# A two-layer block on one core: another order on ScalarE in the first normalisation, and query and key rows stored three deep in stack order

## The chip, the cores and the metric

The kernel runs on one core of a Trainium2 chip. The metric is the device time of one execution in microseconds (us), smaller being better. Before the change the median of three runs is 2131.8 us.

## What is computed

Two layers work on 2 x 512 tokens of width 512 in float32. Layer 0 is an attention with 32 heads of 16 channels and a gated feed-forward network, both on the same normalised input; layer 1 is a state-space mixer and a linear layer with low-rank additions. The change lies at the start of layer 0:

```python
def _layernorm(x, axis=-1, eps=1e-05):
    m = jnp.mean(x, axis=axis, keepdims=True)
    v = jnp.var(x, axis=axis, keepdims=True)
    return (x - m) / jnp.sqrt(v + eps)
...
    q, k, v = (proj(w_q), proj(w_k), proj(w_v))
    scores = jnp.einsum('bhqd,bhkd->bhqk', q, k) / jnp.sqrt(jnp.float32(D_K))
    attn = jax.nn.softmax(scores, axis=-1)
    out = jnp.einsum('bhqk,bhkd->bhqd', attn, v)
...
    xn = _layernorm(x, axis=-1)
    x = x + _L0_attn_ref(xn, ...) + _L0_ffn_ref(xn, ...)
    xn = _layernorm(x, axis=-1)
    x = x + _L1_attn_ref(xn, ...) + _L1_ffn_ref(xn, ...)
```

## The kernel before

The program is five blocks one after the other, each with its own instruction list for every engine: normalisation with the q, k and v products (`emit_qkv`), attention with the gate and up products, the down products with the second normalisation, the state-space mixer, and the output products. Lists are written out by hand, and semaphores alone set when an instruction may run. An engine takes its list in order, so an instruction that waits holds up all behind it. SyncE (SP) issues all the transfers, on one queue.

Float32 products are made of three fp32r products: every operand is split into a high and a low part, and `product` (L154 to L158) adds low x high, high x low and high x high.

**First normalisation** (`FirstNorm`). Tokens come in 8 tiles of 128. For tile t VectorE finds mean and variance (`moments`), ScalarE takes the root (`root`, L217), VectorE makes reciprocal and shift (`scalars`), ScalarE scales the tile (`normalise`, L222), TensorE turns it into PSUM in 4 matmuls (`turn`, L210), ScalarE copies the high part out (`high`, L227) and VectorE the low part (`low`, L255). In step t of ScalarE's list stand root(t), normalise(t-1) and high(t-2), and from step 4 on the split of a weight tile. TensorE's list is: turn 0 to 4, wait for the low part of tile 3, the first 12 products of weight tile 0, turn 5, turn 6, the first 12 products of tile 1, turn 7, wait for the low part of tile 7, and then all other products.

**q, k and v.** There are 12 weight tiles of 256 KB: 8 for q and k in turn (n even is q), then 4 for v. A q or k tile gives 128 channels x 1024 tokens. ScalarE writes its high part to `qk_hi` (`hi`, L503), VectorE its low part to `qk_lo` (L522), both with 3 buffers; then SP writes the two parts of 512 KB each to the scratch tensor `qk_parts` in DRAM (`parts(n)`, L427). ScalarE may fill a buffer again when the writes of the tile three earlier have landed.

**Stacks.** The scores of four heads are made from a stack: two halves of 48 partitions, each of 3 rows of 16 channels (q: high, high, low; k: high, low, high), so that one matmul over 48 partitions adds the three products. `Stacks.stack` (L319) fills one of 4 buffers from `qk_parts` with 12 transfers of 64 KB, one for each row, half and side. There are 16 stacks: 3 are loaded in the first block, right behind `parts(1)`, `parts(2)` and `parts(3)`; the first of them waits until `parts(0)` and `parts(1)` have landed (L432). The others are loaded during attention.

SP's list in the first block is thus: 8 tiles of x, weight tiles 0 to 2, a table of vectors, and then in step n the load of weight tile n and, from n = 6 on, parts(n-6) with the stack behind it. The weights of v (tiles 8 to 11) stand behind parts(1), parts(2), parts(3) and parts(4). At the end come parts(6), parts(7), and two weight tiles of the next block.

TensorE's products of v follow those of q and k: for each of 8 token tiles 12 products, then two row steps (`row_step`, L332; 4 matmuls of L341), from which VectorE takes the row maxima (L351). The first row step waits for the low part of the eighth q/k tile.

Of the kernel before, what the change touches and what calls it, by code (L numbers as in the profile page):

```python
# [13 lines left out]
F32 = mybir.dt.float32  # L14
# [5 lines left out]
P = 128  # L20
B, L, D = 2, 512, 512
T = B * L
KT = D // P
# [52 lines left out]
def after(eng, sem, value):  # L76

    if not isinstance(value, int) or value > 0:
        eng.wait_ge(sem, value)
# [81 lines left out]
class FirstNorm:  # L161
# [66 lines left out]

    def scalar(self, act, feed):
        for t in range(NTOK + 2):  # L230
            if t < NTOK:
                self.root(act, t)
            if 1 <= t <= NTOK:
                self.normalise(act, t - 1)
            if t >= 2:
                self.high(act, t - 2)
            if 4 <= t < 4 + feed.begun:
                feed.split_hi(act, 0, t - 4, 0)

# [55 lines left out]
class Stacks:  # L295
# [23 lines left out]
    def stack(self, sp, c, it, i):  # L319

        n = it * NB + i
        after(sp, self.key_sum, (n - NB + 1) * 16)
        r = it * P + i // 2 * 64
        for row, dst, side, part in ((0, self.qs, 0, 0), (1, self.qs, 0, 0), (2, self.qs, 0, 1),
                                     (0, self.ks, 1, 0), (1, self.ks, 1, 1), (2, self.ks, 1, 0)):
            for half in range(2):
                src = c.qk_rows[part, side, bass.ds(r + half * 2 * DK, 2 * DK), i % 2 * L:(i % 2 + 1) * L]
                at = half * HALF + row * DK
                sp.dma_start(dst[at:at + DK, i, :, :].bitcast(F32),
                             src.rearrange("(h d) t -> d h t", h=2)).then_inc(self.stacked[i], 16)  # L330

    def row_step(self, pe, rows, it, i, u, deep):  # L332

        n = it * NB + i
        if u == 0:
            pe.wait_ge(self.stacked[i], (it + 1) * 12 * 16)
        after(pe, self.max_done, n * 8 + (u - deep + 1))
        qt = u % 4
        for half in range(2):
            at = slice(half * HALF, half * HALF + KSTACK)  # L340
            mm = pe.matmul(rows[:, u % deep, half, :], self.qs[at, i, u // 4, qt * P:(qt + 1) * P],  # L341
                           self.ks[at, i, u // 4, :], start=True, stop=True)
        mm.then_inc(self.row_sum, 1)
# [50 lines left out]
def emit_qkv(nc, c, w, x_load, xhi, xlo, st, feed, tile_done, next_feed):  # L394
# [3 lines left out]
    with ExitStack() as ctx:  # L398
# [23 lines left out]
        @block.sync  # L422
        def _(sp):
            def parts(n):
                sp.wait_ge(qk_l, n + 1)
                for part, src in enumerate((qk_hi, qk_lo)):
                    sp.dma_start(c.qk_dram[part, n % 2 * KT + n // 2], src[:, n % NR, :].bitcast(F32)  # L427
                                 ).then_inc(parts_out[n % NR], 16)
                if n == 1:
                    for s in parts_out[0:2]:  # L430
                        sp.wait_ge(s, 32)
                    sp.wait_ge(st.cleared, 2)  # L432
                if 1 <= n < NB:
                    st.stack(sp, c, 0, n - 1)
            norm.load(sp)
            feed.begin_load(sp)
            norm.load_vectors(sp)
            for n in range(3 * KT):
                if n >= feed.begun:
                    feed.load(sp, w, W_QKV + n, 0, n)  # L440
                if n >= S + 2:
                    parts(n - S - 2)
            for n in range(3 * KT - S - 2, nqk):
                parts(n)
            next_feed.begin_load(sp)
            st.neg_max(sp, 0, 0)
            sp.wait_ge(norm.vec_in, 16)
            for i, s in enumerate(parts_out):
                sp.wait_ge(s, len(range(i, nqk, NR)) * 32)

        @block.tensor
        def _(pe):
# [45 lines left out]
        @block.scalar  # L498
        def _(act):
            def hi(n):  # L500
                act.wait_ge(tile_done, n + 1)
                after(act, parts_out[n % NR], n // NR * 32)
                act.activation(qk_hi[:, n % NR, :], ps[:, n % 3, :, :].rearrange("p b t -> p (b t)"),  # L503
                               ACT.Copy, scale=scale[n]).then_inc(qk_h, 1)
            norm.scalar(act, feed)
            for n in range(3 * KT):
                if n >= feed.begun:
                    feed.split_hi(act, 0, n, n // feed.raw_slots)
                if n >= S:
                    hi(n - S)  # L510
            for t in range(NTOK):
                act.wait_ge(v_sum, t + 1)
                act.activation(v[:, t, :], pv[:, t % 2, :], ACT.Copy).then_inc(v_out, 1)
                if t == HELD:
                    st.high(act, ptr, 0, 0)
                    next_feed.begin_hi(act)
# [1597 lines left out]
def build(nc, w, vec, x_rows, x_out, upto=99):  # L2114
    c = Constants()
    c.vec_dram, c.x_rows = vec, x_rows
    scratch = lambda n, s: nc.dram_tensor(n, s, F32).ap()
    c.qk_dram = scratch("qk_parts", (2, 2 * KT, P, T))
    c.qk_rows = c.qk_dram.rearrange("a (s n) p t -> a s (n p) t", s=2)
    c.att_dram = scratch("att_sums", (2, D, T))  # L2120
    c.x1_dram = scratch("x_mid", (P, KT, T))
    c.cum_dram = scratch("dt_sums", (NTOK, 2, H, CS))
# [100 lines left out]
```

## Time and profile before

| | before |
|---|---|
| median of 3 runs | 2131.8 us (2131.57 to 2133.14) |
| profiled execution, its own time | 2133.82 us |
| its span, first to last instruction | 2132.1 us |
| granted TensorE clock, mean | 0.992 |
| busy: TensorE, VectorE, ScalarE, GpSimd | 98%, 69%, 63%, 41% |
| moved by the DMA engines | 305.34 MB, mean 143 GB/s |

Engines are named as the profile names them: PE is TensorE (PEld its weight loads), DVE VectorE, ACT ScalarE, POOL GpSimd, SP SyncE. A row of the timeline gives the start, the duration, the engine and the source line, the tile written and the tiles read, and in brackets how long the engine had been idle and what ended that. PEclk is the granted clock as a share of 2.4 GHz. The DMA share is the mean busy share of 16 DMA engines. The first block ends at about 107 us of the span, attention at about 400 us.

### The profile page before, as it was taken

To read this page: it belongs to the slowest core of one execution; us is meant where nothing else is said; L and a number is where in the kernel's file an instruction comes from. 1 tells how busy PE (TensorE), PEld (TensorE's weight loads), DVE (VectorE), ACT (ScalarE), POOL (GpSimd) and SP (SyncE) were. 2 spreads that over 40 slices of the span, in tenths; PEclk is the share of its full clock that TensorE was granted. 3 is DMA by queue.
4 is the path that set the end of the run, shared out by engine and by line. 5 is a ranking of instruction groups with operands and counts; after the bars stand their busy time and mean duration, and the time that the engine had idled before them with its cause. 6 is when DMAs were issued, how large, how long until landed. Compare 5 with 4: busy or idle time off the path is not lost.

```text
span 2132.1 us, 33690 instructions
## 1 busy us (share of the span) xinstructions
PE 2081.6 (98%) x12040; PEld 1550.1 (73%) x12040; DVE 1462.3 (69%) x1811; ACT 1337.6 (63%) x2376; POOL 869.6 (41%) x762
## 2 busy tenths in 40 slices
PE   7899999998999999999999999999999999999999
PEld 5644444486777777777777777777777767888887
DVE  4466666285578778778878788687787775555555
ACT  4255555543587877888878787887878783333322
POOL 1011110130157666666757667675766682000000
PEclk9999999999999999999999999999999999999999
DMA  4422222241545555545545545555455467444452
GB/s 158 158 81 74 73 79 62 70 151 55 124 139 166 167 152 163 165 144 171 156 153 171 161 149 161 158 164 161 155 159 167 149 190 257 153 148 148 144 183 89
DMA packets 182781, 305.34 MB, mean 143 GB/s; under 512 B 20416, under 2 KB 96704, under 8 KB 182496
## 3 DMA queue, kind: packets, MB, share of 16 engines
q1 hardware_dynamic: 182624, 303.29, 45.8%
q8 instruction: 94, 1.54, 0.3%
q14 instruction: 63, 0.52, 0.1%
HBM read 249.90 MB, written 53.06 MB: 142 GB/s over the span
## 4 chain that ended last, share of the span: by engine, by line
PE 71%; ACT 2%; DVE 1%; POOL 1%; issue 1%; DMA 1%; DVEq 0%; SPq 0%; POOLq 0%; ACTq 0%
PE ssm_pp L156 16%; PE ssm_pp L158 15%; PE ssm_pp L157 15%; PE ssm_py L1444 5%; PE ssm_py L1439 4%; PE ssm_pstate L1423 4%; PE ssm_turn L1400 2%; PE ssm_py L158 1%; PE ssm_py L157 1%; PE ssm_py L156 1%; PE ssm_pp L1383 1%; PE ssm_pstate L158 1%; PE ssm_pstate L157 1%; PE ssm_pstate L156 1%; PE ssm_turn L158 1%; PE ssm_turn L157 1%
## 5 line engine op out<-in xcount | busy, mean ns | idle before, releaser
L156 PE MATMUL ssm_pp<-xhi,ssm_lo 128*128 128x512 f32 x1192 | 479.4, 402 | 4.2 <-DVE ssm_bc L1668 3.5
L158 PE MATMUL ssm_pp<-xhi,ssm_hi 128*128 128x512 f32 x1192 | 466.0, 391 | 0.0
L157 PE MATMUL ssm_pp<-xlo,ssm_hi 128*128 128x512 f32 x1192 | 465.7, 391 | 0.0
L1556 ACT ACTIVATE ssm_sct<-ssm_cumb,ssm_gpar 128x128 f32<-128x128 f32 x1024 | 313.1, 390 | 72.0 <-DMA ssm_cumb<-dt_sums 48.7
L148 POOL TENSOR_TENSOR ssm_lo<-ssm_raw,ssm_hi 128x512 fp32r<-128x512 f32 x150 | 244.1, 1633 | 92.5 <-ACT ssm_hi L137 92.5
L156 PEld LDWEIGHTS ssm_pp<-xhi,ssm_lo 128*128 128x128 f32 x1192 | 224.0, 188 | 67.5 <-issue 18.7
L1668 DVE SCALAR_TENSOR_TENSOR ssm_xc<-ssm_pp,vectors,ssm_xc 128x1022 f32<-128x1022 f32 (+2 forms) x192 | 245.2, 1277 | 36.2 <-ACT ssm_xc L1510 31.5
L158 PEld LDWEIGHTS ssm_pp<-xhi,ssm_hi 128*128 128x128 f32 x1192 | 224.2, 188 | 48.2
L157 PEld LDWEIGHTS ssm_pp<-xlo,ssm_hi 128*128 128x128 f32 x1192 | 224.3, 188 | 42.7
L1703 DVE TENSOR_TENSOR ssm_sct<-ssm_sct,ssm_cbm 128x1024 f32<-128x1024 f32 x128 | 228.4, 1785 | 27.7 <-ACT ssm_sct L1563 27.7
L1845 POOL TENSOR_TENSOR ssm_go<-ssm_t,ssm_gt 128x512 f32<-128x512 f32 x128 | 165.0, 1289 | 172.1 <-DVE ssm_t L1739 172.1
L767 ACT ACTIVATE att_pt<-att_keys 128x512 f32<-128x512 f32 x256 | 143.9, 594 | 136.0 <-PE att_keys L657 135.8
L2035 ACT ACTIVATE xlo<-ssm_gt 128x1024 fp32r<-128x1024 f32 x64 | 67.8, 1060 | 238.9 <-PE ssm_turn L158 228.1
L351 DVE TENSOR_REDUCE stk_mx<-att_rows 128x2 f32<-128x1024 f32 x112 | 137.3, 1226 | 90.5 <-PE att_rows L341 90.5
L148 POOL TENSOR_TENSOR ffn_lo<-ffn_raw,ffn_hi 128x512 fp32r<-128x512 f32 x33 | 42.9, 1301 | 375.8 <-ACT ffn_hi L137 375.8
L1715 DVE TENSOR_TENSOR ssm_xp<-ssm_turn,ssm_gpar 128x512 f32<-128x512 f32 x128 | 87.8, 686 | 151.2 <-PE ssm_turn L1400 151.2
L1444 PE MATMUL ssm_py<-ssm_sct,ssm_xp 128*64 128x128 f32 x2048 | 184.3, 274 | 0.0
L2072 DVE TENSOR_TENSOR xlo<-ssm_gt,xlo 128x1024 fp32r<-128x1024 f32 x64 | 78.4, 1225 | 149.2 <-ACT xlo L2035 149.2
L1822 POOL TENSOR_TENSOR ssm_xw<-ssm_xp,ssm_gpar 128x512 f32<-128x512 f32 x96 | 127.2, 1325 | 110.3 <-DVE ssm_xp L1715 110.2
L1439 PE MATMUL ssm_py<-ssm_cecl,ssm_state 128*64 128x128 f32 x1536 | 154.1, 279 | 0.1
L1739 DVE SCALAR_TENSOR_TENSOR ssm_t<-ssm_xc,vectors,ssm_py 128x128 f32<-128x128 f32 x512 | 142.4, 336 | 5.3 <-PE ssm_py L1444 5.3
L1444 PEld LDWEIGHTS ssm_py<-ssm_sct,ssm_xp 128*64 128x64 f32 x2048 | 124.5, 137 | 24.3 <-DVE ssm_xp L1715 18.2
(287 smaller groups left out, 4151.4 us busy)
## 6 DMA issues: line engine op xcount, KB each, us to landing
ssm_cumb<-dt_sums SPq DMA_DIRECT2D x96, 1024.0 KB, 5.9
ssm_raw<-w SPq DMA_DIRECT2D x150, 256.0 KB, 5.6
gated<-ssm_go SPq DMA_DIRECT2D x128, 256.0 KB, 4.3
ssm_cumb<-dt_sums SPq DMA_DIRECT2D x32, 512.0 KB, 4.0
ssm_gt<-w SPq DMA_DIRECT2D x64, 256.0 KB, 2.7
ssm_xc<-gated SPq DMA_DIRECT2D x32, 512.0 KB, 4.2
ssm_sct<-gated SPq DMA_DIRECT2D x32, 512.0 KB, 4.3
ffn_raw<-w SPq DMA_DIRECT2D x37, 256.0 KB, 2.8
```

The costliest lines, as they stand in the source:

```text
L148: i = dve.tensor_tensor(lo, src, hi, ALU.subtract)
L156: pe.matmul(out, wlo, xhi, start=start, stop=False)
L157: pe.matmul(out, whi, xlo, start=False, stop=False)
L158: return pe.matmul(out, whi, xhi, start=False, stop=stop)
L767: act.activation(pt[:, kt % 2, PAIRED[u % HQ], :], keys[:, u % 2, :], ACT.Exp).then_inc(exp_done, 1)
L1439: pe.matmul(p_y[r * HP:(r + 1) * HP, s % 2, ct, :], state[:, ch % 2, h * HP:(h + 1) * HP], cecl[:, s % 2, h, :], start=True, stop=False)
L1444: mm = pe.matmul(p_y[r * HP:(r + 1) * HP, s % 2, ct, :], xp[:, s % 2, h * HP:(h + 1) * HP], sct[:, s % 2, h, :], start=(ch == 0), stop=True)
L1556: i = act.activation(sct[:, s % 2, h, :], cumb[:, s % 2, 0, h, :], ACT.Relu, scale=-1.0, bias=gpar[:, unit, 0, s % NTOK, h:h + 1])
L1668: i = dve.scalar_tensor_tensor(dst[:, :, sh:L], pp[:, e % 2, :, 0:L - sh], col(conv_col(g, e) + tap), dst[:, :, sh:L], ALU.mult, ALU.add)
L1703: dve.tensor_tensor(sct[:, s % 2, :, :], sct[:, s % 2, :, :], cbm[:, s % NTOK, :].unsqueeze(1).broadcast_to([P, HU, CS]), ALU.mult).then_i ...
L1739: i = dve.scalar_tensor_tensor(t2[:, s % 2, ct, :], xc[:, s // NTOK, ct, t * CS:(t + 1) * CS], col(g * (2 * CU) + (V_D + s // NTOK * CU + ...
L1845: pool.tensor_tensor(go[:, s % 2, :, :], t2[:, s % 2, :, :], gt[:, s // NTOK, :, t * CS:(t + 1) * CS], ALU.mult).then_inc(g_done, 1)
```

## The change

In ScalarE's list of the first normalisation, high(t-2) now stands ahead of root(t) and normalise(t-1). The scratch tensor becomes `(2 * KT, P // DK, 3, DK, T)`: for each tile and head the three rows of the stack lie one behind the other. `parts(n)` writes the high part twice, so 3 writes of 512 KB in place of 2, and a stack is filled by 4 transfers of 192 KB over 48 partitions in place of 12 of 64 KB over 16. Counts that are waited for follow.

```diff
--- before.py
+++ after.py
@@ -228,12 +228,12 @@
 
     def scalar(self, act, feed):
         for t in range(NTOK + 2):
+            if t >= 2:
+                self.high(act, t - 2)
             if t < NTOK:
                 self.root(act, t)
             if 1 <= t <= NTOK:
                 self.normalise(act, t - 1)
-            if t >= 2:
-                self.high(act, t - 2)
             if 4 <= t < 4 + feed.begun:
                 feed.split_hi(act, 0, t - 4, 0)
 
@@ -320,20 +320,19 @@
 
         n = it * NB + i
         after(sp, self.key_sum, (n - NB + 1) * 16)
-        r = it * P + i // 2 * 64
-        for row, dst, side, part in ((0, self.qs, 0, 0), (1, self.qs, 0, 0), (2, self.qs, 0, 1),
-                                     (0, self.ks, 1, 0), (1, self.ks, 1, 1), (2, self.ks, 1, 0)):
+        for side, dst in enumerate((self.qs, self.ks)):
             for half in range(2):
-                src = c.qk_rows[part, side, bass.ds(r + half * 2 * DK, 2 * DK), i % 2 * L:(i % 2 + 1) * L]
-                at = half * HALF + row * DK
-                sp.dma_start(dst[at:at + DK, i, :, :].bitcast(F32),
-                             src.rearrange("(h d) t -> d h t", h=2)).then_inc(self.stacked[i], 16)
+                src = c.qk_heads[side, bass.ds(it * (P // DK) + (i // 2 * HQ + half * 2), 2), :,
+                                 i % 2 * L:(i % 2 + 1) * L]
+                at = half * HALF
+                sp.dma_start(dst[at:at + KSTACK, i, :, :].bitcast(F32),
+                             src.rearrange("h q t -> q h t")).then_inc(self.stacked[i], 16)
 
     def row_step(self, pe, rows, it, i, u, deep):
 
         n = it * NB + i
         if u == 0:
-            pe.wait_ge(self.stacked[i], (it + 1) * 12 * 16)
+            pe.wait_ge(self.stacked[i], (it + 1) * 4 * 16)
         after(pe, self.max_done, n * 8 + (u - deep + 1))
         qt = u % 4
         for half in range(2):
@@ -423,12 +422,12 @@
         def _(sp):
             def parts(n):
                 sp.wait_ge(qk_l, n + 1)
-                for part, src in enumerate((qk_hi, qk_lo)):
-                    sp.dma_start(c.qk_dram[part, n % 2 * KT + n // 2], src[:, n % NR, :].bitcast(F32)
+                for row, src in enumerate((qk_hi, qk_hi, qk_lo) if n % 2 == 0 else (qk_hi, qk_lo, qk_hi)):
+                    sp.dma_start(c.qk_dram[n % 2 * KT + n // 2, :, row, :, :], src[:, n % NR, :].bitcast(F32)
                                  ).then_inc(parts_out[n % NR], 16)
                 if n == 1:
                     for s in parts_out[0:2]:
-                        sp.wait_ge(s, 32)
+                        sp.wait_ge(s, 48)
                     sp.wait_ge(st.cleared, 2)
                 if 1 <= n < NB:
                     st.stack(sp, c, 0, n - 1)
@@ -446,7 +445,7 @@
             st.neg_max(sp, 0, 0)
             sp.wait_ge(norm.vec_in, 16)
             for i, s in enumerate(parts_out):
-                sp.wait_ge(s, len(range(i, nqk, NR)) * 32)
+                sp.wait_ge(s, len(range(i, nqk, NR)) * 48)
 
         @block.tensor
         def _(pe):
@@ -499,7 +498,7 @@
         def _(act):
             def hi(n):
                 act.wait_ge(tile_done, n + 1)
-                after(act, parts_out[n % NR], n // NR * 32)
+                after(act, parts_out[n % NR], n // NR * 48)
                 act.activation(qk_hi[:, n % NR, :], ps[:, n % 3, :, :].rearrange("p b t -> p (b t)"),
                                ACT.Copy, scale=scale[n]).then_inc(qk_h, 1)
             norm.scalar(act, feed)
@@ -2115,8 +2114,8 @@
     c = Constants()
     c.vec_dram, c.x_rows = vec, x_rows
     scratch = lambda n, s: nc.dram_tensor(n, s, F32).ap()
-    c.qk_dram = scratch("qk_parts", (2, 2 * KT, P, T))
-    c.qk_rows = c.qk_dram.rearrange("a (s n) p t -> a s (n p) t", s=2)
+    c.qk_dram = scratch("qk_parts", (2 * KT, P // DK, 3, DK, T))
+    c.qk_heads = c.qk_dram.rearrange("(s n) h r d t -> s (n h) (r d) t", s=2)
     c.att_dram = scratch("att_sums", (2, D, T))
     c.x1_dram = scratch("x_mid", (P, KT, T))
     c.cum_dram = scratch("dt_sums", (NTOK, 2, H, CS))
```

ScalarE, end of the first normalisation; L217 is root, L222 normalise, L227 high, L137 the split of a weight tile. Before:

```order
L137 ACTIVATE qkv_hi<-qkv_raw 128x512
L217 ACTIVATE ln_rstd<-ln_mean_var,eps 128x1
L222 ACTIVATE stk_v<-stk_v,ln_shift,ln_rstd 128x512
L227 ACTIVATE xhi<-qkv_pv 128x4x128
L222 ACTIVATE stk_v<-stk_v,ln_shift,ln_rstd 128x512
L227 ACTIVATE xhi<-qkv_ps 128x4x128 x2
```

and with the change:

```order
L137 ACTIVATE qkv_hi<-qkv_raw 128x512
L227 ACTIVATE xhi<-qkv_pv 128x4x128
L217 ACTIVATE ln_rstd<-ln_mean_var,eps 128x1
L222 ACTIVATE stk_v<-stk_v,ln_shift,ln_rstd 128x512
L227 ACTIVATE xhi<-qkv_ps 128x4x128
L222 ACTIVATE stk_v<-stk_v,ln_shift,ln_rstd 128x512
L227 ACTIVATE xhi<-qkv_ps 128x4x128
```

Between the last weight split and the end, ahead of normalise(6) there now stands high(5), which needs tile 5 turned.

SP's queue, from the load of weight tile 8 to that of tile 9 (`parts(2)` and the second stack between them; sizes are those of the destination). Before:

```order
L129 DMA qkv_raw<-w 128x512
L427 DMA qk_parts<-qk_hi 128x1024
L427 DMA qk_parts<-qk_lo 128x1024
L329 DMA stk_qs<-qk_parts 16x2x512 x6
L329 DMA stk_ks<-qk_parts 16x2x512 x6
L129 DMA qkv_raw<-w 128x512
```

and with the change:

```order
L129 DMA qkv_raw<-w 128x512
L426 DMA qk_parts<-qk_hi 8x16x1024 x2
L426 DMA qk_parts<-qk_lo 8x16x1024
L328 DMA stk_qs<-qk_parts 48x2x512 x2
L328 DMA stk_ks<-qk_parts 48x2x512 x2
L129 DMA qkv_raw<-w 128x512
```

A third write has come in, of a destination whose first count is 8, and 8 fewer transfers stand ahead of the next weights.

## Rows read from the trace of the kernel before

**Rows 1.** The page, part 1: busy time of each engine
```profile
PE 2081.6 (98%) x12040; PEld 1550.1 (73%) x12040; DVE 1462.3 (69%) x1811; ACT 1337.6 (63%) x2376; POOL 869.6 (41%) x762
```

**Rows 2.** Windows: stretch, length, engines' busy time, PEclk, DMA share, GB/s
```profile
30.00:69.50 39.50, 39.50 (x174) 32.54 (x174) 12.01 (x13) 9.29 (x12) 0.00 (x0) 1.00 0.60 196
69.50:76.20 6.70, 2.76 (x9) 1.33 (x8) 3.83 (x4) 3.08 (x4) 0.00 (x0) 0.88 1.04 421
76.20:81.40 5.20, 5.20 (x15) 3.68 (x15) 2.36 (x2) 0.60 (x1) 0.00 (x0) 0.50 1.01 382
...
120.00:360.00 240.00, 238.91 (x1240) 113.93 (x1240) 156.39 (x172) 129.36 (x247) 28.79 (x32) 1.00 0.27 74
```

**Rows 3.** Waits, 30 to 84 us: us in total, times, longest us
```profile
ACT qkv_hi L137 <- DMA qkv_raw<-w: 20.3, 4, 7.9
```

**Rows 4.** Timeline, 69.3 to 77.5 us: start, duration, operation, idle before, releaser
```profile
73.21 0.63 ACT L137 ACTIVATE qkv_hi<-qkv_raw 128x512 fp32r<-128x512 f32 x1 [1.56 <-DMA qkv_raw<-w]
...
74.61 0.79 PE L156 MATMUL qkv_pv<-qkv_hi,xlo 128*128 128x512 f32 x1 [2.12 <-DVE qkv_lo L148]
...
76.19 1.22 PE L341 MATMUL qkv_ps<-stk_ks,stk_qs 48*128 48x512 f32 x4
```

**Rows 5.** Timeline of SP's queue, 33 to 110 us
```profile
35.91 0.34 SPq L427 DMA_DIRECT2D qk_parts<-qk_hi  x1
...
43.65 2.67 SPq L329 DMA_DIRECT2D stk_qs<-qk_parts  x6
46.36 2.76 SPq L329 DMA_DIRECT2D stk_ks<-qk_parts  x6
...
58.98 5.05 SPq L329 DMA_DIRECT2D stk_qs<-qk_parts  x6
...
68.29 1.01 SPq L129 DMA_DIRECT2D qkv_raw<-w  x1
```

**Rows 6.** Timeline, first normalisation, 0 to 30 us
```profile
7.66 0.81 ACT L222 ACTIVATE stk_v<-stk_v,ln_shift,ln_rstd 128x512 f32<-128x512 f32 x1
...
8.67 0.60 ACT L227 ACTIVATE xhi<-qkv_pv 128x512 fp32r<-128x512 f32 x1 [0.21 <-PE qkv_pv L210]
...
17.41 0.81 ACT L222 ACTIVATE stk_v<-stk_v,ln_shift,ln_rstd 128x512 f32<-128x512 f32 x1
...
18.28 1.11 PE L210 MATMUL qkv_pv<-ident,stk_v 128*128 128x128 f32 x4 [2.10 <-ACT stk_v L222]
...
23.50 0.29 ACT L217 ACTIVATE ln_rstd<-ln_mean_var,eps 128x1 f32<-128x1 f32 x1 [1.05 <-DVE ln_mean_var L244]
...
23.86 0.81 ACT L222 ACTIVATE stk_v<-stk_v,ln_shift,ln_rstd 128x512 f32<-128x512 f32 x1
...
24.72 0.66 PE L210 MATMUL qkv_ps<-ident,stk_v 128*128 128x128 f32 x4
24.82 0.60 ACT L227 ACTIVATE xhi<-qkv_pv 128x512 fp32r<-128x512 f32 x1
...
29.96 0.50 PE L156 MATMUL qkv_ps<-xhi,qkv_lo 128*128 128x512 f32 x1 [1.41 <-DVE xlo L255]
```

**Rows 7.** The DMA view of 95 to 103 us
```profile
DMA packets 64, 0.02 MB, mean 2 GB/s; under 512 B 32, under 2 KB 64, under 8 KB 64
...
stk_qs<-stk_nmh SPq DMA_DIRECT2D x2, 4.0 KB
stk_qs<-stk_nml SPq DMA_DIRECT2D x2, 4.0 KB
```

**Rows 8.** DMA view, 34.5 to 84 us: GB/s in 40 slices; packets
```profile
GB/s 0 86 404 341 298 414 371 0 114 147 139 138 141 286 425 372 210 156 147 114 341 424 364 141 109 131 139 162 437 424 404 410 420 420 410 420 334 356 51 0
DMA packets 5044, 12.63 MB, mean 255 GB/s; under 512 B 944, under 2 KB 944, under 8 KB 5040
```

**Rows 9.** Windows, as rows 2, of 72 to 74 us
```profile
72.00:74.00 2.00, 0.49 (x3) 0.05 (x1) 1.04 (x2) 0.79 (x2) 0.00 (x0) 1.00 1.05 423
```

**Rows 10.** The tile view of qk_parts, its last row
```profile
DMA to landing us min/median/max: 2.0/2.2/5.2
```

## The prediction

> **What bounds the kernel now.** I read the busy times first, then the windows stage by stage, then the waits and the timeline of the one stretch that is not full. TensorE is busy 98% of the span [rows 1], so a change pays, or costs, only where TensorE waits or runs at the lower clock. The windows [rows 2] say where that can be. From 30 to 69.5 us it has no gap. From 69.5 to 76.2 us it works 2.76 of 6.70 us, and then 5.2 us go by at a granted clock of 0.50, which is the 1.2 GHz level, after the engine stood idle twice. In the sampled 240 us of attention it works 238.91 us, so faster stack loads can give there at most 1.1 us; I take 0.
>
> The hole at 69.5 us comes from weights. ScalarE waits 20.3 us in 4 waits for weight tiles [rows 3]; the last of them, v's fourth, is split at 73.21, and TensorE takes it up at 74.61 and reaches the first row step at 76.19 [rows 4]. That tile was issued by SP only at 68.29, because it stands behind three stacks of 12 issues; one stack takes 2.67 + 2.76 = 5.4 us of SP's time, and with the engines full up to 5.05 + 2.76 = 7.8 us [rows 5]. So SP's issue time bounds the stage before, by a queue that is late. Two idle stretches and the low clock behind them are what a shorter queue could win back.
>
> **The first normalisation.** At its start the new order costs and then gains. normalise(1) began at 7.66; now it stands behind high(0), which began at 8.67 when tile 0 was turned, and a root: 8.67 + 0.60 + 0.29 = 9.5. From there one tile follows the next by normalise 0.81, turn 1.11, high 0.60 and root 0.29, some 2.8 us less 0.1 of overlap, where it took (17.41 - 7.66) / 3 = 3.25 us. normalise(4) comes at 9.5 + 3 x 2.7 = 17.6 against 17.41 [rows 6]: about even, 0.2 either way, and the first products, which also need turn 4 (18.28), start as before. At the end it costs. Before, normalise(6) ran at 23.86, while TensorE was still in the first 12 products, and turn 6 followed turn 5 at 24.72. Now high(5) stands ahead of it and needs turn 5, which stands behind those products: high at 24.82, then 0.60 + 0.29 + 0.81 less 0.1 of overlap, so turn 6 can start at 26.4. What follows (12 products, turn 7, high, low, and the products from 29.96 [rows 6]) has no slack to take it up: **+1.6 us**, between 0 and 1.8. TensorE's idle time there is then 1.6 us; before, an idle stretch of 1.41 us ahead of 29.96 [rows 6] was followed by full clock from 30 us on [rows 2], so I take no clock loss, with 3.4 us (below) as the other end.
>
> **The issues saved.** For each of three stacks SP issues 8 transfers fewer and 1 write more, at about 0.45 us each (2.67 / 6, [rows 5]): 3.2 us, up to 5.5 us where the engines were full. Weights would be issued that much earlier. This is worth something only if the transfers ahead of them are done earlier too, and that is the next question: what is late next is the DMA engines.
>
> **The third write, and how many engines carry it.** Bytes first. The writes of one q/k tile grow from 1 MB to 1.5 MB. The engines, all 16 busy, move 423 GB/s [rows 9], 26.4 GB/s each. Now the count of engines. Between 34.5 and 84 us the trace has 16 + 36 + 5 + 2 = 59 transfers, and 944 packets under 512 B [rows 8], 16 for each: every engine that takes part leaves one small packet. All 59 have a first count of 16 or 128. The only four transfers from 95 to 103 us have a first count of 8 (1x8x128 with the 1 dropped), and there 64 packets are 32 of 512 B and 32 small ones [rows 7]: 8 engines each. The new write has a destination of 8x16x1024 and a source of 128 partitions. No row shows such a mixed pair; the engines can be 16 or 8. I take 8, from the row whose destination has the same first count. The queue then does not spread a write over all engines, and everything behind it on those 8 engines waits, the weights included, since a weight tile is whole only when all 16 engines have brought their part.
>
> The Trainium skill, "DMA: Bandwidth & Descriptors", section "Why a DMA increments its semaphore by 16 and not by 1", says that the queue takes the largest number up to 16 that divides the slowest count of both sides, and the lowest-numbered engines; for 128 and 8 that is the same 8 engines every time. By that rule the sum is the one below; without it, the 16 of the first rival. The small packets of rows 7 and 8 agree with it as far as they go.
>
> **The sum with 8 engines.** On one of the 8 a write of 512 KB takes 64 KB / 26.4 GB/s = 2.48 us, three of them 7.45; a weight tile over 16 engines 0.62; a stack of 768 KB 1.86. A transfer of 64 KB lands 2.0 us after its issue at best [rows 10] though it moves for 0.16, so I put 0.95 before the first byte and 0.9 behind the last.
> - parts(0) was issued at 35.91 [rows 5]; now 37.5, first byte at 38.45.
> - parts(0), a weight tile, parts(1): 7.45 + 0.62 + 7.45 = 15.5; landed at 54.9. SP waits for that before the first stack, which it issued at 43.65 before [rows 5].
> - First byte of the stack at 55.85. Up to v's fourth weight tile there come 3 stacks, 4 weight tiles and 3 x 3 writes: 5.6 + 2.5 + 22.35 = 30.4 us; landed at 87.2. SP's own issues are far shorter and lie beside this.
> - ScalarE splits that tile at 87.2 in place of 73.21: 14.0 us late. What follows is unchanged, so the first row step is at 90.2 in place of 76.19.
>
> The 1.6 us of the normalisation is inside these 14.0, since the chain starts with the first q/k tile. TensorE waits in v's first tile as before, only longer (some 9 and 7 us), so the clock falls again and costs what it cost, 0.5 x 5.2 = 2.6 us [rows 2]: difference 0, with ends of -0.8 (it comes back sooner after the row step) and +2.6. Behind the last weights 9 writes and two weight tiles of the next block are still queued, 23.6 us; ScalarE splits those behind v's fifth tile, and TensorE may be two tiles ahead of ScalarE's copies: 0, up to +2. **Sum: +14.0 us.** Against the profiled execution (2133.82 us, of which 2132.1 are span) that is 2147.8; this execution is 2.0 us above the median shown, so against the median I forecast **2145.8 us**.
>
> Ends of the sum: nothing lost in the normalisation -1.6, a rate of 27.3 GB/s an engine (437 GB/s, the fastest slice of [rows 8]) -1.5, clock -0.8; SP held up by full engines (issues of 1.0 where 0.45 is usual, [rows 5]) with gaps on the engines up to +3, clock +2.6, next block's weights +2. Alone this case runs from 2142 to 2153; I add 5 us below for engines that run faster while the others idle, which no row shows or excludes.
>
> The same page, section "Specifications", gives about 27 GiB/s for one engine, some 29 GB/s; as an estimate from it the 45.9 us of transfers would be 41.8 and the time 2141.7. The row's 26.4 is measured here and is used.
>
> **Rivals.** (1) *Sixteen engines, or halves that take turns: faster.* The trace has no mixed pair, which speaks for it; rows 7 speak against. Then a write takes 1.24 us, the weights land before they are needed, and both idle stretches go. v's first tile would end at 69.5 + 6 products of 0.23 (39.50 / 174, [rows 2]) = 70.9; the low part of the last q/k tile comes 76.19 - 73.21 = 2.98 us [rows 4] after the tile's end at 68.1 (6 products before 69.5), at 71.1. With 1.6 the row step is at 72.7: -3.5, and the low clock goes, -2.6: 2131.8 - 6.1 = **2125.7**. The point that decides is the engine count of one write. (2) *Sixteen engines, and the clock lost earlier: no change.* If the 1.6 us gap after 24.8 drops the clock for as long as here (74.6 to 81.4 us, at half rate 3.4 us), it is **2129.1**, inside 0.2%. For it: the clock had only just risen in this stretch. Against: the 1.41 us gap that changed nothing. (3) *Eight engines and everything late: slower still.* The next block's weights hold ScalarE's copies of v (+2) and the early clock falls (+3.4): **2151**. For it, 23.6 us of transfers still queued; against, two tiles ahead.
>
> **How the numbers follow.** 0.2% of the time, 4.3 us, is about what a measurement of this kernel can tell from no change. Eight engines: 0.83, of which 0.08 for rival 3, all slower by more than that. Sixteen engines or turns: 0.10 faster. Rival 2, or eight engines of which much is absorbed: 0.07 same. The range of 2137 to 2154 holds nearly all of the eight-engine case, its 0.83 less some 0.03 of tails, and ends above both others; to hold more it would have to reach 2126.
>
> **What would show it.** Right: from 40 to 85 us a DMA share near 0.5 at some 210 GB/s; 8 small packets for one write; the first stack issued near 55; v's fourth weight tile split near 87; first row step near 90; turn 6 some 1.6 us after turn 5; attention as full as before. Wrong: 16 small packets for a write and a share near 1, the row step near 73 with the clock up, then rival 1. If the writes are on 8 engines but the weights land by 76, my reading that they queue behind the writes is wrong; if the row step is at 90 and the time is not 14 us up, the slack lies in attention, which the windows deny.

## The result, and the profile after

The change made the kernel **slower by 20.4 us**: 2152.89 us median of 4 runs (2152.62 to 2155.36) against 2132.47 (2131.57 to 2133.69) before, a ratio of 1.0094 with a 95% interval of 1.0081 to 1.0107. The forecast was 14.0 us slower, 2145.8 with a range of 2137 to 2154. The profiled execution after took 2152.89 us, 2151.2 of it span.

TensorE's busy time is what it was, so the loss is waiting. From the page's part 1 of the changed kernel, to be read against [rows 1]:

```profile
PE 2080.7 (97%) x12040; PEld 1549.5 (72%) x12040; DVE 1465.6 (68%) x1811; ACT 1336.7 (62%) x2376; POOL 870.6 (40%) x762
```

The windows of the changed kernel, columns as in [rows 2], tell where:

```profile
30.00:69.50 39.50, 33.26 (x147) 27.04 (x145) 10.71 (x12) 8.84 (x12) 0.00 (x0) 0.99 0.45 137
...
81.40:102.60 21.20, 5.58 (x14) 3.10 (x14) 5.77 (x7) 3.68 (x5) 0.00 (x0) 0.52 0.54 211
140.00:380.00 240.00, 238.92 (x1239) 114.24 (x1237) 157.22 (x173) 129.97 (x248) 28.80 (x32) 1.00 0.31 74
```

The stretch from 30 to 69.5 us, full before, has 6 us of holes (most of it the idle 5.15 us that end at 69.82 below); from 81.4 to 102.6 TensorE works 5.6 of 21.2 us, at the 1.2 GHz level nearly throughout; attention is as full as before. In the second row the DMA engines are at a share of 0.54 and 211 GB/s, where the kernel before ran at 1.04 and 421 in its hole. ScalarE's waits, 34 to 110 us, against [rows 3], and from its timeline its splits of v's first and fourth weight tile:

```profile
ACT qkv_hi L137 <- DMA qkv_raw<-w: 46.6, 5, 13.2
```

```profile
66.87 0.63 ACT L137 ACTIVATE qkv_hi<-qkv_raw 128x512 fp32r<-128x512 f32 x1 [13.21 <-DMA qkv_raw<-w]
...
97.34 0.63 ACT L137 ACTIVATE qkv_hi<-qkv_raw 128x512 fp32r<-128x512 f32 x1 [6.47 <-DMA qkv_raw<-w]
```

And the timeline of TensorE from 69 us, to be read beside [rows 4]:

```profile
69.82 0.77 PE L156 MATMUL qkv_ps<-xhi,qkv_lo 128*128 128x512 f32 x1 [5.15 <-DVE qk_lo L521]
...
80.51 0.50 PE L156 MATMUL qkv_pv<-qkv_hi,xlo 128*128 128x512 f32 x1 [1.72 <-DVE qkv_lo L148]
...
90.74 0.80 PE L156 MATMUL qkv_pv<-qkv_hi,xlo 128*128 128x512 f32 x1 [9.26 <-DVE qkv_lo L148]
...
98.75 0.80 PE L156 MATMUL qkv_pv<-qkv_hi,xlo 128*128 128x512 f32 x1 [6.36 <-DVE qkv_lo L148]
...
100.33 1.22 PE L340 MATMUL qkv_ps<-stk_ks,stk_qs 48*128 48x512 f32 x4
```

Weight tiles came late. ScalarE takes its list in order, so its 13.21 us of waiting for v's first tile also held up its copies of q/k tiles. It split v's fourth tile at 97.34 us against 73.21. The first row step is 24.1 us late. On like instructions the two traces are 22.2 to 22.4 us apart in attention. At the end they are 19.1 apart: 0.8 came back near 520 us, and 2.4 where the execution before had a clock fall near 1775 us that this one lacks.

The DMA view of the changed kernel, 34.5 to 59.5 us, shows why the weights were late (GB/s in 40 slices; then packets):

```profile
GB/s 0 26 0 0 0 13 0 98 85 52 105 105 125 138 197 193 275 324 203 190 164 164 115 167 197 197 216 210 210 210 210 210 210 210 210 177 118 105 52 13
DMA packets 962, 3.43 MB, mean 137 GB/s; under 512 B 64, under 2 KB 64, under 8 KB 960
```

It holds 6 writes and one weight tile. Their 64 packets under 512 B are 6 x 8 + 16: each write was on 8 engines. In the plateau at 210 GB/s, which is 210 / 8 = 26.3 GB/s for each of the 8 engines, the windows give a share of 0.51; the forecast used 26.4. By the Trainium skill, "DMA: Bandwidth & Descriptors", section "Why a DMA increments its semaphore by 16 and not by 1", these are the same lowest-numbered engines each time. The trace agrees that they are the same ones, since the share stays at 0.51 with several writes queued; it does not show which. SP's queue, against [rows 5]:

```profile
37.68 1.47 SPq L426 DMA_DIRECT2D qk_parts<-qk_hi  x2
39.20 2.67 SPq L426 DMA_DIRECT2D qk_parts<-qk_lo  x1
...
59.73 0.81 SPq L328 DMA_DIRECT2D stk_qs<-qk_parts  x2
60.59 0.91 SPq L328 DMA_DIRECT2D stk_ks<-qk_parts  x2
...
83.50 1.00 SPq L129 DMA_DIRECT2D qkv_raw<-w  x1
```

The first stack, 4 transfers, now costs SP 1.7 us in place of 5.4, as hoped for, but it is issued 16 us later.

### The profile page after: what moved, and what is told of

The parts are those of the page before. It is cut to its first block, busy times and chain, and to the rows that moved or that the text cites. A ratio compares the mean times of both kernels' runs of the same rounds, so it can differ in the third digit from the quotient of the medians.

```text
span 2151.2 us, 33472 instructions
## 1 busy us (share of the span) xinstructions
PE 2080.7 (97%) x12040; PEld 1549.5 (72%) x12040; DVE 1465.6 (68%) x1811; ACT 1336.7 (62%) x2376; POOL 870.6 (40%) x762
## 3 DMA queue, kind: packets, MB, share of 16 engines
q1 hardware_dynamic: 181536, 307.47, 46.6%
## 4 chain that ended last, share of the span: by engine, by line
PE 70%; ACT 2%; DVE 1%; POOL 1%; issue 1%; DMA 0%; DVEq 0%; SPq 0%; POOLq 0%; ACTq 0%
PE ssm_pp L156 16%; PE ssm_pp L158 15%; PE ssm_pp L157 15%; PE ssm_py L1443 5%; PE ssm_py L1438 4%; PE ssm_pstate L1422 4%; PE ssm_turn L1399 2%; PE ssm_py L156 1%; PE ssm_py L158 1%; PE ssm_py L157 1%; PE ssm_pp L1382 1%; PE ssm_pstate L156 1%; PE ssm_pstate L158 1%; PE ssm_pstate L157 1%; PE ssm_turn L156 1%; PE ssm_turn L158 1%
```

## The experiments

The diffs below show the lines that decide; counts and shapes that follow from them are left out. The theory was that the loss is the eight engines of a write, with everything that queues behind them. Its rivals were the bytes of the third write, the wide stack transfers, ScalarE's new order, and the order of SP's queue. All the runs, each against the kernel before as run beside it (medians 2132.5 to 2133.6 us); the two columns on the right are from each kernel's one profiled execution, in us:

| run | time, us | ratio (95%) | first stack issued | first row step |
|---|---|---|---|---|
| before | | | 43.65 | 76.19 |
| the change | 2152.89 | 1.0081 to 1.0107 | 59.73 | 100.33 |
| new order of ScalarE alone | 2132.05 | 0.9992 to 1.0010 | 44.11 | 76.45 |
| storage alone | 2155.29 | 1.0084 to 1.0119 | 57.87 | 98.54 |
| change, 16 engines | 2135.57 | 1.0007 to 1.0026 | 49.77 | 82.04 |
| before, 2 writes on 8 engines | 2150.90 | 1.0067 to 1.0104 | 53.02 | 96.78 |
| before, third write on 16 | 2137.49 | 1.0010 to 1.0028 | 46.57 | 83.06 |
| storage alone, 16 engines | 2136.01 | 1.0002 to 1.0021 | 48.96 | 79.92 |
| before, weights first | 2130.66 | 0.9976 to 0.9994 | 43.78 | 73.26 |
| change, weights first | 2155.29 | 1.0089 to 1.0120 | 59.10 | 97.38 |
| storage, 16 engines, stacks late | 2126.91 | 0.9964 to 0.9983 | 48.76 | 71.88 |
| before, stacks late | **2124.21** | 0.9950 to 0.9977 | 43.87 | 71.40 |
| change, stacks late | 2152.94 | 1.0081 to 1.0112 | 59.79 | 93.82 |
| the 16-engine one with narrow stacks | 2133.75 | 0.9993 to 1.0012 | 48.48 | 75.61 |

**The two halves of the change.** The first run is the kernel before with the diff's first hunk alone, the second is the change without that hunk.

```diff
+if t >= 2:
+    self.high(act, t - 2)
 if t < NTOK:
     self.root(act, t)
 if 1 <= t <= NTOK:
     self.normalise(act, t - 1)
-if t >= 2:
-    self.high(act, t - 2)
```

> Only ScalarE's new order in the first normalisation. Theory A (the gap between turn 5 and turn 6 passes on to the end): the products of the second half start at 31.7 us in place of 29.96, and the kernel is 1.6 to 1.8 us slower than before, 2134.2 us. Rival: the later wait for v's weights takes the 1.8 us up, since SP's queue is late anyway; then under 0.5 us.

> The storage, the three writes and the four transfers a stack, with ScalarE's old order. Theory A (eight engines for each write): first row step near 98.5 us where it is 100.33 with the whole change, 2151 us. Rival: the two parts work on each other and the storage alone costs less than 15 us, under 2147 us.

The timeline of TensorE in the first of them, and then in the changed kernel, 21 to 33 us:

```profile
21.84 0.40 PE L157 MATMUL qkv_ps<-xlo,qkv_hi 128*128 128x512 f32 x1
22.07 0.40 PE L158 MATMUL qkv_ps<-xhi,qkv_hi 128*128 128x512 f32 x1
...
23.00 0.60 PE L210 MATMUL qkv_pv<-ident,stk_v 128*128 128x128 f32 x4
25.17 0.66 PE L210 MATMUL qkv_ps<-ident,stk_v 128*128 128x128 f32 x4 [1.57 <-ACT stk_v L222]
...
30.41 0.50 PE L156 MATMUL qkv_ps<-xhi,qkv_lo 128*128 128x512 f32 x1 [1.41 <-DVE xlo L255]
```

```profile
23.12 0.63 PE L156 MATMUL qkv_ps<-xhi,qkv_lo 128*128 128x512 f32 x1
23.55 0.63 PE L157 MATMUL qkv_ps<-xlo,qkv_hi 128*128 128x512 f32 x1
...
26.45 0.66 PE L210 MATMUL qkv_ps<-ident,stk_v 128*128 128x128 f32 x4 [1.57 <-ACT stk_v L222]
...
31.74 0.50 PE L156 MATMUL qkv_ps<-xhi,qkv_lo 128*128 128x512 f32 x1 [1.41 <-DVE xlo L255]
```

The gap ahead of turn 6 is there, 1.57 us, the same as in the changed kernel. But the products behind it start only 0.45 us later than in the kernel before (30.41 against 29.96), where the changed kernel is 1.78 late. The difference is when the clock rose from 1.2 to 2.4 GHz: at 22 us products already follow each other by 0.23 us here, while at 23.1 us in the changed kernel they still do so by 0.43. Over all the traces of this study, with either order, the rise comes between 21.5 and 24.9 us. The 0.45 us was not taken up later either: this execution is 0.8 us behind the one before at the second row step and 1.4 at the end. The median, 2132.05, is no change, but its interval reaches from 1.7 us faster to 2.1 slower, and the 1.6 to 1.8 us of theory A lie inside it. So this run decides neither for theory A nor for its rival.

The storage alone gives the whole loss: 2155.29 where 2151 was expected, with the row step where it was expected. Between the change and the storage alone the gap is visible at the first row step (100.33 against 98.54) and mostly gone at the second (104.98 against 104.53): without it TensorE reaches the row step earlier, but the 2.4 GHz level returns later, at 103.8 against 102.6 us. The windows from 98 to 105 us show it, first of the change, then of the storage alone, where the granted clock averages 0.67 and 0.59:

```profile
98.00:105.00 7.00, 6.25 (x21) 3.94 (x21) 4.27 (x4) 1.48 (x2) 0.00 (x0) 0.67 0.51 210
```

```profile
98.00:105.00 7.00, 7.00 (x22) 4.36 (x20) 2.71 (x3) 0.96 (x2) 0.00 (x0) 0.59 0.51 209
```

**Sixteen engines for the same writes.** The q and k weights' columns were set out so that a tile's partitions run over the head's channel first, and the destination's first count became 16:

```diff
-sp.dma_start(c.qk_dram[n % 2 * KT + n // 2, :, row, :, :], ...
+sp.dma_start(c.qk_dram[n % 2 * KT + n // 2, :, row, :, :].rearrange("h d t -> d h t"), ...
```

> The whole change, but the channels of a q/k tile lie channel-major (rows of w_q and w_k permuted in the layout of the weights), so that each of the three writes has a destination of 16x8x1024. Theory A (the count of engines is the cause): 16 small packets for each write, writes at over 350 GB/s, both waits in v's first tile gone or under 1 us, first row step at 73 us, 2126 us. Rival B (the bytes of the third write and the wide stack transfers are the cause, on however many engines): row step after 85 us, over 2140 us.

From 34.5 to 49.7 us the 6 writes and one weight tile of this run leave 112 packets under 512 B, 6 x 16 + 16: each write is on 16 engines. Of the 20.4 us, 17.4 went (3.0 are left, 2135.57 against 2132.6). That is the engines' count; the same rows of memory are written as in the change, in another order, so where they lie is not the loss. But the gain that 16 engines should have brought (2126 us, row step at 73) did not come either. The window from 40 to 70 us shows the new bound, the DMA engines themselves; the second row is the same window of the kernel before:

```profile
40.00:70.00 30.00, 30.00 (x134) 24.86 (x133) 7.66 (x8) 6.18 (x8) 0.00 (x0) 1.00 0.95 292
```

```profile
40.00:70.00 30.00, 29.70 (x132) 24.24 (x130) 7.67 (x8) 6.19 (x8) 0.00 (x0) 1.00 0.69 228
```

**Eight engines without the rest.** The kernel before, with one padding row behind each head in memory, so that its two writes have the destination 8x16x1024; stacks stay 12 narrow transfers:

```diff
-c.qk_dram = scratch("qk_parts", (2, 2 * KT, P, T))
+c.qk_dram = scratch("qk_parts", (2, 2 * KT, P // DK, DK + 1, T))
```

> The kernel before, its two writes and 12 transfers a stack kept, but with one unused row behind each head in the scratch tensor, so that the destination of a write is 8x16x1024. Theory A: 8 small packets for a write, a DMA share of 0.5 while only writes run, first stack issued 5 to 8 us later than 43.65, first row step 8 to 18 us later than 76.19, about 2144 us. Rival B (bytes): same bytes, so the row step stays at 76 to 78 and the time at 2132 to 2134 us.

From 34.5 to 53 us 4 writes and one weight tile leave 48 packets under 512 B, 4 x 8 + 16. Two writes on 8 engines cost nearly what the whole change does: +18.3 us (two executions), first stack 9.4 us late where 5 to 8 were expected, row step 20.6 late where 8 to 18 were. The bytes are those of before, so it is the engines' count and not the third write. One reason that it is more than the theory's sum, not separated from others, is that 8-engine writes begin slowly, as in the changed kernel: in the DMA view of this run from 34.5 to 48 us the rate stays between 24 and 190 GB/s for the first 4 us of writing.

```profile
GB/s 0 0 0 0 24 0 0 0 0 133 97 73 85 24 133 85 97 97 146 176 188 394 261 170 158 134 182 206 121 115 109 225 182 194 188 212 200 225 206 194
```

**The bytes, and the width of the stack reads.** The kernel before with a third write on 16 engines to memory that nobody reads; and the 16-engine storage with ScalarE's old order:

```diff
-for part, src in enumerate((qk_hi, qk_lo)):
+for part, src in enumerate((qk_hi, qk_lo, qk_hi)):
```

> The kernel before with a third 512 KB write of each q/k tile (the high part again, to scratch that nobody reads), its destination 128 partitions wide and so on 16 engines; stacks stay 12 narrow transfers. It measures the bytes of the third write alone. Theory (the engines' count is the loss, the bytes are minor): a write takes 1.24 us on 16 engines and 0.45 us to issue; 3 to 4 of them lie ahead of v's fourth weight tile, so the row step comes 3 to 6 us late (79 to 82 us in place of 76.2) and the time is 2134 to 2139. Rival (the third write as such is the loss, wherever it runs): row step past 90 us, 2146 or more. Second rival (with 16 engines it is hidden): 2131 to 2133.

> The run with 16 engines (third write, 4 wide transfers a stack, q/k channels reordered so that the destination is 16x8x1024), but with ScalarE's old order in the first normalisation. Theory: the 12 wide transfers of the three stacks cost the engines what the 36 narrow ones cost SP, so it ends 0 to 2 us below the run with the new order: 2133.5 to 2135.5, row step near 81 us against 82.04. Rival (the new order is the 3 us that the run with 16 engines was above the kernel before): 2130 to 2132.5, row step at or before 78. Against the run with a third write and narrow stacks it tells what width of a stack's read costs: equal bytes, so whichever has the earlier row step has the cheaper reads.

The third write's bytes cost 3.9 us and 6.9 at the row step (0.9 past the upper end of the theory's 3 to 6). At equal bytes, 4 wide transfers in place of 12 narrow ones, with the new form of the writes, are worth 3.1 us at the row step of one trace each and 1.5 in time. The time of that run, 2136.01, is 0.5 above the theory's range, beside a kernel before that was itself 1.0 higher than in the earlier runs. So on this one path from the change back to before the 20.4 us divide into: eight engines 17.4, third write 3.9, wide transfers -1.5, ScalarE's order 0.6 (2135.57 against 2136.01, each less its own kernel before). The last two are within the noise, as the intervals overlap widely, and the parts need not be the same by another path: on 8 engines the change is not above the storage alone.

**Where the weights stand on SP's queue.** The same edit to the kernel before and to the changed one: loads of v's weight tiles ahead of the stacks.

```diff
+for n in range(S + 4, 3 * KT):
+    feed.load(sp, w, W_QKV + n, 0, n)
+    if n >= S + 5:
+        stack(n - S - 4)
+        parts(n - S - 3)
```

> The kernel before, with SP's queue alone reordered: v's first two weight tiles ahead of the first stack, the third ahead of the second, the fourth ahead of the third; bytes, issues and engines unchanged. Theory (TensorE's hole at 69.5 us of the kernel before is v's weight tiles standing behind stacks on SP's queue, and the clock fall follows from the hole): v's fourth tile is split near 70 in place of 73.21, the row step comes at 72 to 74 in place of 76.19, the clock does not fall at 74.7 us, and the time is 2125 to 2129. Rival A (the splits wait for buffers or the hole is the last q/k tile's low part): row step at 75 or later and 2130 to 2133. Rival B (writes and stacks pushed back by the weights hold q/k buffers): slower, 2134 to 2138.

> The change whole, with SP's queue reordered in the same way (v's weight tiles ahead of stacks). Theory (the 8 engines that carry all writes are the bound, 7.45 us a q/k tile against 5.4 us of TensorE, so order can't save them; the q/k buffers, of which there are three, then hold the last tiles): at most 3 to 7 us of the 20 come back, row step at 93 to 98 us, time 2145 to 2150. Rival (the loss is only that v's weights stand behind writes and stacks): v's fourth tile split near 80, row step at 80 to 86, time 2130 to 2138.

On the kernel before it gains 3.0 us: 2130.66 where the theory had 2125 to 2129, with the row step inside its 72 to 74. ScalarE no longer waits for a weight, but for the buffer of the last q/k tile, TensorE waits 2.26 us and the clock still falls. ScalarE's wait, and then TensorE's row step, in the timeline of that run:

```profile
70.92 1.02 ACT L509 ACTIVATE qk_hi<-qkv_ps 128x1024 fp32r<-128x1024 f32 x1 [1.92 <-DMA qk_parts<-qk_lo]
...
73.26 0.73 PE L341 MATMUL qkv_ps<-stk_ks,stk_qs 48*128 48x512 f32 x4 [2.26 <-DVE qk_lo L528]
```

On the changed kernel it gains nothing; not even the 3 to 7 us that the theory allowed. The weights' waits fall from 46.6 to 14.4 us and reappear as waits for the writes that must free a buffer. The waits of ScalarE in that run, 30 to 125 us:

```profile
ACT qk_hi L508 <- DMA qk_parts<-qk_lo: 20.6, 2, 12.0
...
ACT qkv_hi L137 <- DMA qkv_raw<-w: 14.4, 3, 7.5
ACT qk_hi L508 <- DMA qk_parts<-qk_hi: 9.1, 1, 9.1
```

**Stacks late.** Next, the second stack behind tile 4's writes and the third behind tile 5's, for three kernels: the storage on 16 engines, the kernel before, and the changed one.

```diff
+st.stack(sp, c, 0, 1)
+parts(nqk - 3)
+st.stack(sp, c, 0, 2)
+parts(nqk - 2)
```

> The run with 16 engines and ScalarE's old order, with SP's queue reordered: v's weight tiles and the writes of q/k tiles 2 to 4 ahead of the second stack, the third stack behind the sixth tile's writes. Theory (with 16 engines the third write costs only where a weight tile or a q/k buffer stands behind full engines): with v's weights landed in time and writes of 3.7 us a tile against 5.4 us of TensorE, the row step comes at 71 to 74 us where it was near 80, and the time is 2127 to 2131. Rival (the bytes of the third write cost whatever their place): row step at 76 or later, 2132 to 2136.

> The kernel before with SP's queue reordered further than in the run with the weights first: the second stack behind the writes of q/k tile 4, the third behind tile 5's, v's weight tiles ahead of both; bytes, issues and engines unchanged. In the run with the weights first ScalarE still waited 1.92 us for a write (the buffer of the last q/k tile), TensorE 2.26 us for its low part, and the clock then fell. Theory: that wait goes, the row step comes at 71 to 72 us (73.26 there, 76.19 before), TensorE's wait there is under 1 us, and the time is 2126 to 2130. Rival (the stacks then come too late, for row step 8 or for the first step of attention): a wait of TensorE near 88 or 103 us, and the time is at or above the run with the weights first, 2130 to 2134.

> The change whole with this second order of SP's queue (stacks two and three behind the writes). Theory (8 engines carry 7.45 us of writes a q/k tile; the buffer of the last tile comes free when tile 4's writes have landed): one stack, 5 tiles and 6 weight tiles from 38.4 us on give 82, and with the slow first writes and stack seen in the change 88 to 92; row step at 88 to 94 us against 100.33, time 2141 to 2147. Rival (the engines are not the bound, the queue's order is): row step at 71 to 80, 2128 to 2135. Second rival (as with the weights first, nothing comes back): 2150 or more.

The second of them is the fastest kernel of the study, 8.5 us below the kernel before. Its hole is gone; windows with the columns of [rows 2]:

```profile
69.50:76.20 6.70, 6.47 (x30) 4.30 (x29) 4.64 (x5) 1.78 (x3) 0.00 (x0) 1.00 0.65 213
76.20:81.40 5.20, 5.20 (x24) 3.77 (x23) 3.94 (x4) 0.60 (x1) 0.00 (x0) 1.00 1.00 358
```

TensorE works 6.47 of 6.70 us where it worked 2.76, and the granted clock stays at 1.00 behind it, where it was 0.50. The time is below the 2126 to 2130 of the theory. The shift against the kernel before is -4.8 us at the first row step and -7.2 at the second: 2.4 of it is the clock. The profiled execution ends 11.3 us earlier, 2.4 of it because it lacks the clock fall near 1775 us; the medians are 8.5 apart. The storage on 16 engines with this order takes 2126.91, 5.8 us below its kernel before, where without the order it was 2.4 above. The change on its 8 engines gains nothing in time. Its row step comes at 93.82, as the theory said (88 to 94), but by the second row step 1.5 of those 6.5 us are gone again, ScalarE then waits 6.9 us for the next block's weights (3.3 in the change), and 2152.94 is the second rival's number, not the 2141 to 2147 of the theory. In none of the three orders of SP's queue that were tried do 8 engines get the stage's transfers done in time.

**Narrow reads of the new storage.** The 16-engine kernel with late stacks, each stack read by 12 transfers:

```diff
-sp.dma_start(dst[at:at + KSTACK, i, :, :].bitcast(F32), src.rearrange("h q t -> q h t"))
+for row in range(KSTACK // DK):
+    at = half * HALF + row * DK
+    sp.dma_start(dst[at:at + DK, i, :, :].bitcast(F32), src[:, row * DK:(row + 1) * DK, :].rearrange("h d t -> d h t"))
```

> The run with 16 engines and late stacks, with each stack read from the new storage by 12 transfers of 16 partitions in place of 4 of 48. It tells whether the slow packets of the stack reads (2 KB in 0.14 to 0.17 us, where the kernel before has 0.084 in the median) hang on the storage or on the wide transfers. Theory (wide transfers): 2 KB packets of the first stack, from 49 to 54 us, back at 0.084 in the median and the DMA rate per unit of busy share near 290 GB/s, as from 44.5 to 48 us of the kernel before (136 at 0.46), against 199 at 1.03 in the run with 16 engines. Rival (the order of the rows in memory): 0.14 us or more at the median whatever the width. The time is 2126 to 2131 either way, since SP's issues (2.67 + 2.76 us a stack) are no longer ahead of a weight tile.

On the packets the theory held: in the packet records from 49 to 53 us 2 KB take 0.084 us in the median, as in the kernel before, where they take 0.139 in the run with late and wide stacks (weight tiles, also in 2 KB packets, are among them). The windows of the first stack agree: first 50.5 to 53.5 us of the storage on 16 engines (wide), then 49.5 to 54 of this run (narrow):

```profile
50.50:53.50 3.00, 3.00 (x15) 2.49 (x14) 0.00 (x0) 0.00 (x0) 0.00 (x0) 1.00 1.03 199
```

```profile
49.50:54.00 4.50, 4.50 (x22) 3.72 (x21) 1.13 (x2) 1.54 (x2) 0.00 (x0) 1.00 0.50 141
```

199 / 1.03 = 193 GB/s for a full share against 141 / 0.50 = 282. On the time it missed: 2133.75, 6.8 us above the wide form. The first stack holds SP 5.4 us in place of 1.7, and the next weight tile is issued at 53.99 us in place of 50.56. TensorE then waits 3.28 us ahead of the row step (0.90 in the wide form), and ScalarE 5.9 us for the next block's weights (0.5). The wide form is slower on the engines and still the better one. What makes its packets slow, the 48 partitions or the number of engines at work at once, was not separated.

## Why the prediction was right, and where its sum fell short

- **What bounds the kernel**: right. The weights on SP's queue made the hole at 69.5 us: moving the stacks alone, with no byte or issue less, closed it and gave 8.5 us.
- **The first normalisation, +1.6 us**: the mechanism and the size were right at its place (turn 6 waits 1.57 us, products at 31.74 against 29.96). How late the products then start also hangs on when the clock rises, which the forecast left out: 0.45 us in the run with the new order alone. As a cost of the kernel it stays open: the new order's runs alone and at 16 engines differ from the old order's by less than their noise. With 8 engines the 1.8 us are still there at the first row step and mostly gone at the second, where the clock came back earlier.
- **Engines of a write**: 8, as taken from the row with the same first count, and 26.3 GB/s each. The figure of the Trainium skill, same page, section "Specifications" (some 29 GB/s an engine), was not reached, and its estimate of 2141.7 is the further off. This step carried the forecast, and the runs with 16 and with 8 engines show it as the cause of 17.4 of the 20.4 us.
- **The sum with 8 engines**: mis-sized. The row step was put at 90.2 and came at 100.33. Of the 10.1 us, 4.8 lie in "landed at 54.9": SP issued the first stack at 59.73. The first writes ran at 52 to 138 GB/s for some 4.4 us, not at 8 x 26.4 = 211, which is about half of it; the rest is slower stretches behind them and an end at falling rate. The other 5.3 lie between that issue and the row step, and no run splits them. "A stack of 768 KB 1.86" is the likeliest term: in the window of 60 to 64.5 us the changed kernel moves 170 GB/s at a share of 0.83, with a weight tile and the next writes beside the first stack. At that rate a stack takes 4.6 us; three would add 8.3, of which part would lie beside other work. The 1.86 took its rate from a stretch of contiguous writes and a weight tile [rows 9].
- **The range**: the time lies 1.1 us inside its upper end, and that is partly luck. The row step missed by more than the range allowed for, and had the 22 us of attention reached the end, the time would have been above 2154; 3.2 us of them came back in places that the forecast did not look at.
- **Clock, 0 (-0.8 to +2.6)**: about right. After the row step 1.4 us came back (second row step +22.8 against +24.1), somewhat more than the -0.8 allowed. The forecast had no fall ahead of v's products; there was one (products 0.43 us apart from 70.38 to 74.65 us), and it cost nothing, since TensorE then waited for weights anyway.
- **Next block's weights, 0 (up to +2)**: right; ScalarE waits 3.3 us for them at 120 us and TensorE's row steps still follow each other by some 3.62 us.
- **Attention, 0**: right, 238.92 of 240 us.
- **Rivals**: the first was priced at 2125.7 for 16 engines. The run gave 2135.57: the sum there had the weights land before they are needed, but ScalarE waits 24.9 us for them, with the engines at a share of 0.95. With the stacks late and ScalarE's old order it is 2126.91, near that price, by another route. The second's condition, a clock lost behind the 1.6 us gap, did not come in the changed kernel: it stays at 2.4 GHz from 24.1 to 68.5 us. The third's price, 2151, is the nearest to the time, but by luck: neither of its two terms came.

## What to carry to other kernels

Before a tensor is stored in a new shape, count the engines that each write will use from the small packets of transfers with the same outer counts: half the engines cost far more here than the issues saved. Where a load of weights and a bulk transfer share one issuing queue, first ask which of them is needed first; the reorder was worth 8.5 us and changed no byte. A rate read from one form of transfer need not hold for another: take each from a row of its own form, or keep both ends. And look in the trace whether a delay put in early is still there at the end before calling it absorbed: one early clock rise can hide it.

## What the runs showed of the hardware that was not expected

- 8-engine writes to strided rows begin slowly: 24 to 190 GB/s for the first 4 us in the run with two writes; the changed kernel comes to a steady 210 at a share of 0.51 only at 51 us. The first writes of the 16-engine form do so too, at 85 to 243 GB/s for some 1.7 us, while contiguous writes of the same tile reach 388 within 0.7 us. The engines are not idle in it: from 38.9 to 43.3 us of the changed kernel the share is 0.47 at 103 GB/s, and a tenth of its 4 KB packets take some 0.65 us or more, where the median is 0.159. Why was not tried.
- From 49 to 53 us, 2 KB pieces take 0.139 us a packet in the median with stack reads 48 partitions wide, and 0.084 with reads 16 wide. Four issues in place of 12 saved SP time and cost the engines.
- SP's own issue of a write took up to 2.67 us in the changed kernel (39.20 us), where those of the kernel before take 0.33 to 1.18.
- The rise of TensorE's clock in the first products moves by 3.4 us from one execution to another (21.5 to 24.9 us), so one trace of a kernel does not price a change at that place.
